# Attention strip of a two-layer graph network: f32 turns set singly among PV tiles, the 256-column product last in a tile, and the ELU's last two additions moved from GpSimd to VectorE

## The reference

```
q = h @ Wq.T + bq;  k = h @ Wk.T + bk;  v = h @ Wv.T + bv
scores = q @ k.T / sqrt(128);  scores = where(adj > 0, scores, -9e15)
att = softmax(scores) @ v
x = x + elu(att)
```

## Time and profile before

| | |
|---|---|
| time, median of 3 runs | 761.54 us (760.59 to 762.22) |
| the profiled execution's own time | 758.33 us |
| its span | 756.5 us |
| TensorE busy, matmuls | 724.9 us, 96% of the span |
| VectorE busy | 558.8 us, 74% |
| ScalarE busy | 549.0 us, 73% |
| GpSimd busy | 448.9 us, 59% |
| mean granted clock of TensorE | 0.975 |

### The profile page before, as it was taken

The page is one execution under the profiler, slowest core; times in us unless marked ns, Lnnn a source line. Parts: engine busy times, 40 slices in busy tenths (PEclk is TensorE's granted clock), DMA queues, the critical chain, the costliest instruction groups (busy, mean ns, idle before and its releaser), DMA issues. The chain is left out here.

```text
span 756.5 us, 18346 instructions
## 1 busy us (share of the span) xinstructions
PE 724.9 (96%) x6243; PEld 616.0 (81%) x6243; DVE 558.8 (74%) x1190; ACT 549.0 (73%) x1090; POOL 448.9 (59%) x388
## 2 busy tenths in 40 slices
PE   7989999999999999999999998989799999999996
PEld 5567878888888888888888887887688888888885
DVE  6979787887878778787787877578387477577572
ACT  4745868778786877878777787676986887887810
POOL 6688699999999999999999989470000000000000
PEclk9999999999999999999999999758999999999999
DMA  6299899998989889898898943783234542442100
GB/s 236 99 290 223 252 272 232 281 255 247 258 236 282 244 261 251 250 270 233 277 257 246 260 110 65 135 110 100 62 82 86 85 96 63 94 92 65 38 10 12
DMA packets 193307, 132.71 MB, mean 175 GB/s; under 512 B 174064, under 2 KB 180720, under 8 KB 184944
## 3 DMA queue, kind: packets, MB, share of 16 engines
q1 hardware_dynamic: 192528, 131.90, 65.6%
q10 hardware_dynamic: 576, 0.26, 0.1%
q0 software_dynamic: 160, 0.00, 0.0%
HBM read 71.31 MB, written 18.89 MB: 119 GB/s over the span
## 5 line engine op out<-in xcount | busy, mean ns | idle before, releaser
L898 DVE CUSTOM_DVE_ANT_0 scores<-ps_s,mask_both 128x1024 f32<-128x1024 f32 x128 | 155.8, 1217 | 17.4 <-POOL mask_both L350 17.4
L770 ACT ACTIVATE scores<-scores,neg_max 128x1024 f32<-128x1024 f32 x128 | 146.0, 1142 | 25.9 <-DVE neg_max L904 25.9
L917 DVE TENSOR_TENSOR low<-scores 128x1024 bf16<-128x1024 f32 x96 | 140.1, 1459 | 30.4 <-ACT scores L770 30.4
L350 POOL TENSOR_SCALAR mask_both<-mask_bytes 128x2048 bf16<-128x2048 uint8 x64 | 153.3, 2396 | 5.4 <-POOL mask_bytes L345 0.4
L345 POOL TENSOR_SCALAR mask_bytes<-adj_both 128x2048 uint8<-128x2048 int32 x64 | 148.3, 2336 | 2.9 <-DMA adj_both<-in_adj 2.0
L1152 PE MATMUL spare<-v_parts,hiT 128*128 128x256 bf16 x768 | 140.3, 273 | 1.6 <-DMA lowT<-low 1.6
L784 ACT ACTIVATE hiT<-spare 128x512 bf16<-128x512 bf16 (+1 forms) x128 | 103.0, 805 | 50.9 <-PE spare L1133 48.3
L1153 PE MATMUL spare<-v_parts,lowT 128*128 128x128 bf16 x768 | 133.5, 219 | 0.0
L1584 PE MATMUL ps_x<-q_parts,over_k 128*128 128x258 bf16 x1024 | 117.4, 276 | 3.6 <-issue 3.6
L1584 PEld LDWEIGHTS ps_x<-q_parts,over_k 128*128 128x128 fp8e4 x1024 | 99.8, 98 | 19.2 <-issue 3.7
L1106 PE MATMUL ps_s<-k_hi,q_strip 128*128 128x512 f32 x256 | 112.4, 439 | 2.1 <-PEq L81 1.9
(11 more groups left out here) (174 smaller groups left out, 1280.2 us busy)
## 6 DMA issues: line engine op xcount, KB each, us to landing
adj_both<-in_adj SPq DMA_DIRECT2D x64, 1024.0 KB, 5.3
mask_bytes_dram<-mask_bytes SPq DMA_DIRECT2D x32, 512.0 KB, 2.9
x_sb<-in_x SPq DMA_DIRECT2D x8, 256.0 KB, 6.8
out<-res SPq DMA_DIRECT2D x32, 64.0 KB, 1.6
lowT<-low SPq DMA_TRANSPOSE x96, 4.8
mask_both<-s_row_dram SPq DMA_DIRECT2D x1, 1024.0 KB, 7.6
mask_both<-s_row_dram SPq DMA_DIRECT2D x1, 768.0 KB, 11.4
over_k<-mask_bytes_dram SPq DMA_TRANSPOSE x16, 4.6
```

The costliest lines, as they stand in the source:

```text
L350: return nc.gpsimd.tensor_scalar(out, src, -NEG, NEG, ALU.mult, ALU.add)
L770: nc.scalar.activation(sc, sc, ACT.Exp, bias=neg_max[:, bn:bn + 1], accum_out=row_sum[:, bn, k:k + 1]).then_inc(exp_done, 1)
L898: nc.vector.tensor_tensor_reduce(out=scores[bn % 2][:, part(k)], in0=ps_s[k % 2][:], in1=mask[bn % 2][:, part(k)], scale=1.0, scalar=LOWES ...
L917: nc.vector.tensor_tensor(low[k][:], p, high_half(p), ALU.subtract).then_inc(low_done, 1)
```

## The change

On TensorE, `turn` takes the products of the strip before into itself where there is one (`times_before`): each of the four f32 turns is followed by the two products of one tile. The waits of those products (`wait_for_part`, formerly in `times_v`) stand ahead of the first turn. `t_done` is still given by the fourth turn, behind which one tile's products follow. In every tile but the first of a strip the 128-column product now comes first and the 256-column one last. On GpSimd `add_elu` keeps one addition, exp + positive part, and gives a new semaphore `elu_ready`. VectorE gets `add_x`, (that sum - 1) + x in one instruction, between `moments_of(s-3)` and `low_part(s+1, 0)`; it gives `epi_done`.

```diff
--- before.py
+++ after.py
@@ -520,7 +520,7 @@
             halves_added, att_ready, att_cut = sem("acc_halves_added"), sem("att_ready"), sem("att_cut")
             att_exp_ready, epi_done = sem("att_exp_ready"), sem("epilogue_done")
             m_stored = [sem("even_masks_stored"), sem("odd_masks_stored")]
-            own, pool_own = sem("vector_steps"), sem("pool_steps")
+            own, elu_ready = sem("vector_steps"), sem("elu_ready")
             sp_gate, pool_gate = sem("sync_gate"), sem("pool_gate")
             bn_done, tail_own = sem("moments_taken"), sem("tail_vector_steps")
             h_ready, h_by_vector = sem("h_ready"), sem("h_by_vector_ready")
@@ -684,12 +684,8 @@
 
                     def add_elu(s):
 
-                        steps = Steps(pool, pool_own, 2 * s)
                         pool.wait_ge(att_exp_ready, s + 1)
-                        steps.do(nc.gpsimd.tensor_tensor(att_exp[:], att_exp[:], ones[:], ALU.subtract))
-                        steps.do(nc.gpsimd.tensor_tensor(att_exp[:], att_exp[:], att_pos[:], ALU.add))
-                        xs = x_sb[:, s, :] if isinstance(s, int) else x_sb[:, bass.ds(s, 1), :].rearrange("p o f -> p (o f)")
-                        nc.gpsimd.tensor_tensor(xs, xs, att_exp[:], ALU.add).then_inc(epi_done, 1)
+                        nc.gpsimd.tensor_tensor(att_exp[:], att_exp[:], att_pos[:], ALU.add).then_inc(elu_ready, 1)
 
                     make_bytes(0, 1)
                     make_mask(0, 1)
@@ -923,6 +919,13 @@
                         wait(dve, acc_out, s - 1)
                         nc.vector.reciprocal(inv_by_parity[:, b % 2:b % 2 + 1], inv_sum[:, b % 2:b % 2 + 1]).then_inc(inv_ready, 1)
 
+                    def add_x(s):
+
+                        dve.wait_ge(elu_ready, s + 1)
+                        xs = x_sb[:, s, :] if isinstance(s, int) else x_sb[:, bass.ds(s, 1), :].rearrange("p o f -> p (o f)")
+                        nc.vector.scalar_tensor_tensor(out=xs, in0=att_exp[:], scalar=-1.0, in1=xs,
+                                                       op0=ALU.add, op1=ALU.add).then_inc(epi_done, 1)
+
                     def moments_of(s):
 
 
@@ -1041,6 +1044,8 @@
                         if has(c, b, -3):
                             dve.wait_ge(epi_done, s - 2)
                             moments_of(s - 3)
+                        if has(c, b, -2):
+                            add_x(s - 2)
                         if isinstance(c, int) and s == T - 3:
                             dve.wait_ge(var_made, 1)
                             first_guess(FIRST)
@@ -1055,6 +1060,7 @@
                     inverse_sum(T - 1, 3)
                     dve.wait_ge(epi_done, T - 2)
                     moments_of(T - 3)
+                    add_x(T - 2)
                     dve.wait_ge(epi_done, T - 1)
                     moments_of(T - 2)
                     aggregate(slice(LAST.start, T - 1))
@@ -1108,14 +1114,22 @@
                             last = nc.tensor.matmul(o, rest, k_hi[:, col], start=False, stop=True)
                         last.then_inc(s_ready, 1)
 
-                    def turn(s, b, i):
+                    def turn(s, b, i, times_before):
+
 
                         pe.wait_ge(exp_done, 4 * s + 1)
-                        wait(pe, hiT_ready, 4 * (s - 1) + 2 + i)
+                        if times_before:
+
+                            wait_for_part(s - 1, 6 + i)
                         for t in range(4):
                             col = 512 * (6 + i) + D * t
-                            last = nc.tensor.transpose(ps_t[i % 3][:, D * t:D * t + D], scores[b % 2][:, col:col + D], ident[:])
-                        last.then_inc(t_done, 1)
+                            turned = nc.tensor.transpose(ps_t[i % 3][:, D * t:D * t + D], scores[b % 2][:, col:col + D], ident[:])
+                            if t == 3:
+                                turned.then_inc(t_done, 1)
+                            if times_before:
+                                last = tile_times_v(6 + i, t)
+                        if times_before:
+                            last.then_inc(pv_done, 1)
 
                     def turn_high(s, b, u):
 
@@ -1133,7 +1147,7 @@
                             last = nc.tensor.transpose(out[:, D * t:D * t + D], high[:, D * t:D * t + D], ident_half[:])
                         last.then_inc(t_done, 1)
 
-                    def times_v(s, i):
+                    def wait_for_part(s, i):
                         j = PV_ORDER[i]
                         if i < 2:
                             pe.wait_ge(pT_low_ready, 2 * s + i + 1)
@@ -1143,15 +1157,32 @@
                                 pe.wait_ge(lowT_in[j // 2], 16 * s + 16)
                         if i == 0:
                             wait(pe, acc_out, s)
+
+                    def tile_times_v(i, n):
+
+
+                        j = PV_ORDER[i]
+                        t = 4 * j + n
+                        first, final = i == 0 and n == 0, i == NC - 1 and n == 3
+                        if j >= 6:
+                            high, rest = (m[j - 6][:, D * n:D * n + D] for m in (pT_high, pT_low))
+                        else:
+                            high, rest = hiT[j // 2][:, D * (t % 8):D * (t % 8) + D], lowT[j // 2][:, t % 8, :]
+
+                        def times_low():
+                            return nc.tensor.matmul(ps_a[:, 0, :], rest, v_parts[:, t, 0, :], start=False, stop=False)
+
+                        if not first:
+                            times_low()
+                        last = nc.tensor.matmul(ps_a[:], high, v_parts[:, t, :, :], start=first, stop=final)
+                        if first:
+                            last = times_low()
+                        return last
+
+                    def times_v(s, i):
+                        wait_for_part(s, i)
                         for n in range(4):
-                            t = 4 * j + n
-                            if j >= 6:
-                                high, rest = (m[j - 6][:, D * n:D * n + D] for m in (pT_high, pT_low))
-                            else:
-                                high, rest = hiT[j // 2][:, D * (t % 8):D * (t % 8) + D], lowT[j // 2][:, t % 8, :]
-                            nc.tensor.matmul(ps_a[:], high, v_parts[:, t, :, :], start=(i == 0 and n == 0), stop=False)
-                            last = nc.tensor.matmul(ps_a[:, 0, :], rest, v_parts[:, t, 0, :], start=False,
-                                                    stop=(i == NC - 1 and n == 3))
+                            last = tile_times_v(i, n)
                         last.then_inc(pv_done, 1)
 
                     for k in range(NP):
@@ -1162,19 +1193,15 @@
                     def period(c, b):
                         s = 4 * c + b
                         before, ahead, ahead2 = has(c, b, -1), has(c, b, 1), has(c, b, 2)
-                        turn(s, b, 0)
+                        turn(s, b, 0, before)
                         if not ahead:
                             pe.wait_ge(masked, 4 * T)
                             turn_h(0)
-                        if before:
-                            times_v(s - 1, 6)
                         if ahead:
                             make_scores(s + 1, 1 - b % 2, 2)
-                        turn(s, b, 1)
+                        turn(s, b, 1, before)
                         if not ahead:
                             turn_h(1)
-                        if before:
-                            times_v(s - 1, 7)
                         if ahead:
                             make_scores(s + 1, 1 - b % 2, 3)
                         turn_high(s, b, 0)
```

## The result

The changed kernel takes **777.46 us** (median of 4 runs, 774.8 to 781.6), the kernel before beside it 761.88 (760.59 to 763.1): a ratio of **1.0209**, 95% interval 1.0171 to 1.0247. It is slower, clear of the noise, but the interval begins at 1.7%, so that it is not shown to be slower by as much as 2%. The prediction was 781.5 us with a range of 774 to 787, 88% on slower. The profiled execution took 781.6 us, with a span of 779.8 against 756.5 before.

A forecast was written before the change was run, and what follows sets the result against it. TensorE's gapless work and an equally long ScalarE-VectorE-ScalarE loop, 13.35 us a period, were taken as the bound; +21.6 - 0.8 - 0.8 = +20.0 on the median 761.54 gave 781.5 us, range 774 to 787.

The forecast's parts named there:

- Two loops of one length: Attention stage: the loop ScalarE to VectorE to ScalarE is as long as TensorE's period, 13.35 us.
- Who starts first holds the other: VectorE's subtraction against GpSimd's instruction: the first to start runs, the other stands; a held subtraction ends 1.07 us after.
- rival 1: VectorE keeps its turn: low_part(s,1) stays ahead of the mask half, TensorE sets 13.13 a period, 753.3 us; chance 8%.
- The loop, +0.77 a period: VectorE's loop: low_part(s,1) held, +1.25; low_part(s,2) freed, -0.48; over 28 periods +21.6 us.
- `add_x` worth 0 on the loop: VectorE's added instruction costs between 0.28 and 0.28 + 1.90 us, covered by 1.8 of idle time: 0.
- TensorE's waits: TensorE, with 0.99 us over a period, waits some 0.8 to 1 us for the second pT_low.
- The products' order, 0.22 a period but hidden: TensorE: the 256-column product last covers the scores' f32 load, 0.22 us a period, worth nothing under the longer loop.
- The single turns, worth 0: TensorE's f32 turns: each lasts 0.11 us itself, so spreading them saves 0; if load-bound, 0.44 a period.
- The end of the stage, -0.8 and -0.8: Last strips: ScalarE's wait for att goes, -0.8; shorter GpSimd additions before VectorE's moments, -0.8.
- Rival 2: VectorE keeps its turn and turns are load-bound: TensorE needs 12.69, the loop of 12.87 sets the pace, 746.5 us; chance 2%.
- Rival 3: add_x costs as well: 0.2 us a period, 787 us; worst, it and low_part(s+1,0) both held, +59; chance 8%.
- Rival 4: GpSimd's late work lengthens the loop only every other period: +9.2, 770.7 us; chance 4%.

The follow-up runs named there:

- Number 7: The changed kernel with TensorE's order as before the change and two GpSimd waits, behind turned_low(s,0) and behind low_part(s+1,0): 758.21 us, ratio 0.9948.
- Number 2: Only the TensorE part of the change (single turns, 256-column product last), add_elu as in the kernel before: 759.3 us, ratio 0.9966.
- number 4: The changed kernel with two unneeded 128x128 instructions on GpSimd around the remaining addition, so its mask half starts later: 784.64 us, ratio 1.0291.
- number 3: The changed kernel with one more GpSimd wait: the first mask half waits until VectorE has done turned_low(s,0): 767.24 us, ratio 1.0074.
- number 6: Number 5 with the four f32 turns issued together again, the 256-column product still last in a tile: 755.15 us, ratio 0.9898.
- number 1: Only the GpSimd and VectorE part of the change, TensorE's order as in the kernel before: 782.19 us, ratio 1.0241.
- number 5: Number 3 with a second GpSimd wait: the second bytes half waits until VectorE's low_part(s+1,0) is done: 753.39 us, ratio 0.9888.

## Why the prediction was right, point by point

**Two loops of one length.** Right. Number 7 leaves TensorE's work as it was and frees the loop: 13.34. Number 2 shortens TensorE's work and leaves the loop: 13.30. The period before was 13.34, so the loop lay 0.04 under TensorE's need. TensorE alone could give only 0.04 a period, and a longer loop had to show in full.

**Who starts first holds the other.** Right, and it carried the result. `low_part(s,1)` ends 1.07 after the mask half, the figure taken from the earlier trace rows, and the second mask half 1.76 after the subtraction (244.12 against 242.36). In the Trainium skill, SBUF — State Buffer, the section "SBUF: two separate sides" says the same as a rule: an exclusive lock between a GpSimd instruction that reads SBUF and a VectorE instruction with two SBUF inputs, which whoever starts first keeps for the whole instruction. The ten traces agree but for ties. A subtraction or `add_x` starts inside a mask half or bytes half, with 0.2 us or more of it left, 445 times in them. It is held 443 times, the closest with GpSimd 0.042 us ahead. The other two are the meetings of number 4 at 0.015 and 0.012 us, which VectorE won. So VectorE does win near ties, as rival 1 supposed, but nowhere from 0.042 us on; in the changed kernel GpSimd leads by 0.49.

**The loop, +0.77 a period.** Measured 0.734 (20.55 / 28). Of the two terms, the hold was worth +1.26 (2.48 against 1.22) for +1.25, and the freed `low_part(s,2)` -0.49 for -0.48. Walked through as the prediction walked it, the loop of period 13 is 0.61 + 0.61 + 4.15 + 2.56 + 0.03 + 6.11 = 14.07, so the other small difference is ScalarE's stretch, 6.11 where it was 6.16. Once in four periods (s = 12, 16 and so on, behind the loop's jump) the hold is 2.23 instead of 2.48, with a period of 13.84 behind one of 14.29; the two together are as long as any other two.

**`add_x` worth 0 on the loop.** Right in its effect. Its price within the bounds of 0.28 and 2.18 came out at 1.77, near the upper one. I had GpSimd's bytes halves at 194.9 and 196.8 and left open which one is met; it was the second. The cover held: `low_part(s+1,0)`, behind it, had stood 0.85 for ScalarE before and 0.2 in a hold, and now has neither. The exclusion of "both are held" was right for this kernel by a margin that the prediction did not state. Numbers 3 and 4 show how thin: the first bytes half starts 7.4 us behind the first copy in the changed kernel, 8.4 in a period of number 4 with the double hold and 9.0 in number 3.

**TensorE's waits.** Foreseen 0.8 to 1 us a period in front of the second `pT_low`; the table has 23.1 us in 28 waits, 0.83 each. GpSimd's wait for `att_exp` was to be 2 to 3 us and was 3.1.

**The products' order, 0.22 a period but hidden.** Right on both counts: 0.22 in number 6 against 7, and next to nothing (number 1 against after, 14.07 against 14.08) under the longer loop. The sign that the prediction gave for it was wrong: the second scores product was to start 0.28 to 0.30 behind the last product of a tile, and it is 0.34 (201.24 to 201.58 in number 5, 244.73 to 245.07 in the changed kernel). The prediction's own durations, 0.11 for a 256-column product and 0.23 for the first scores product, give 0.34.

**The single turns, worth 0.** Right, 0.016 a period in number 6. The rule of the Trainium skill that the prediction weighed against the row, TensorE: Matmul & The Clock Gate, section LDWEIGHTS, would have made it 0.44. Four turns in a row can't tell a turn's own time from that of its load. Set singly, each turn's load has a 256-column product to stand behind, and the pace is still 0.11 us: it is the turn's own.

**The end of the stage, -0.8 and -0.8.** Measured -0.96 from strip 30 to 31, where the row of ScalarE's wait for `att` is gone, and -1.14 from strip 31 to the last `att`. The terms were mis-sized by 0.2 and 0.3, both on the side that I took too small.

**The rest.** Two stretches that the prediction took as unchanged are not: +2.5 us in the first two periods and +1.9 in the second layer. The first holds one 4.3 us wait of TensorE for `lowT` (in the table of waits above). It is scatter of the opening. `add_elu` and `add_x` first come in period 2, so number 1 has the instructions of the kernel before in these two periods, and took 31.29 us for them against 28.45; number 4 has those of the changed kernel, and took 26.32 against 30.96. The second is in a stage where no instruction differs, and there too the ten executions scatter, from 274.4 us (number 1) to 276.8 (numbers 2 and 7), again not by kernel. Part of it is the clock. The same two stretches of 20 us, counted from the last `att`, before (from 60.2 us behind it) and after (columns as in the earlier trace rows):

```profile
542.00:562.00 20.00, 15.09 (x124) 12.46 (x123) 15.85 (x28) 17.69 (x33) 0.00 (x0) 0.91 0.26 58
```

```profile
563.35:583.35 20.00, 15.09 (x111) 11.92 (x110) 15.78 (x28) 16.18 (x30) 0.00 (x0) 0.83 0.26 57
```

TensorE gets through 124 matmuls before and 111 after, at a granted clock of 0.91 and 0.83: in both it idled for 4.9 us of the 20, and came back to full clock later in the second (in its four stretches of 5 us the clock is 1.00, 0.66, 1.00, 1.00 before and 1.00, 0.51, 0.81, 1.00 after). That is scatter that no term of a sum can hold; a profiled execution differs from another by 2 us for it.

**The size as a whole.** The forecast of +20.0 us is that of the profiles, less their scatter: loop and tail together are +18.45. The medians say +15.6, and the interval of the ratio reaches from 13.0 to 18.8, so +20.0 lies a little above it and the 20.55 of the loop less the tail's gains just inside. Of the 4.4 us by which the medians fall short of +20.0, the loop's term (21.6 against 20.55) and the tail's (1.6 against 2.1) make 1.5. The other 2.9, between 18.45 and 15.6, can't be placed, since the unprofiled runs have no trace; number 1, with the same loop to 0.01 us a period, had +20.3.

**The rivals.** None came in the changed kernel. Rival 1's time, 753.3, is what number 5 gives (753.39), but by two ordering waits and not by the 0.5 us of delay that the rival named as its point. Rival 2 falls with the single turns. Rival 3's worst order appears in number 3, but at 13.68 a period, 0.8 above the 12.87 of rival 1's loop, where the rival had 2.1. `add_x` and the hold of `low_part(s+1,0)` come to 1.89 + 1.68 = 3.6 there and not 4.1. And the prediction's 1.8 us of idle time leaves out a third piece, in front of the mask that follows the maximum. Before the change and in number 3 (where the `gate` is that mask's first step):

```profile
195.36 1.22 DVE L898 CUSTOM_DVE_ANT_0 scores<-ps_s,mask_both 128x1024 f32<-128x1024 f32 x1 [0.73 <-POOL mask_both L350]
```

```profile
200.02 0.06 DVE L894 MEMSET gate<- 128x1 f32 x1 [0.20 <-PE spare L1148]
```


VectorE stood 0.73 us there for GpSimd's mask and now stands 0.20. That leaves some 0.3 of the difference unplaced. Rival 4's alternation appears in number 4, which is worse than the rival had it: not one free period and one lengthened by 1.5, but one near 13.0 and one of 15.3 to 16.4.

## What to carry to other kernels

Work taken from an engine that shares something with the one on the critical path is a change of phase before it is a saving: list where the two meet, who starts first at each meeting and by how much, and redo that list with the new times. Where a meeting matters, order it by a wait on the engine that has time to spare; two such waits turned this change from +2.1% into -1.1%. When one meeting is moved, look at the next: number 3 repaired the first and lost at the second.

## What the runs showed of the hardware that was not expected

- A 128x128 `SCALAR_TENSOR_TENSOR` with both inputs in SBUF is held as fully as the large subtraction: 0.28 us free, 1.77 in the changed kernel, 1.89 in number 3. Here a small instruction put between large ones of the other engine cost 1.6 of the 1.9 us that one of theirs takes.
- Starting first by the trace's stamps does not decide at the very closest: at leads of 0.015 and 0.012 us GpSimd's mask half was held by the subtraction behind it (number 4), at 0.042 and more it never was. No meeting lies between.
- Holding feeds back. In number 4 short and long periods follow each other (12.98 and 15.28, 13.03 and 16.35) though every period issues the same instructions: an early subtraction makes GpSimd late, which makes the next subtraction late.
- Two executions can differ by 4.6 us in the opening (26.3 and 31.0 us for the first two periods) and by 2.4 in the second layer (274.4 to 276.8 us) with the same instructions there. The medians of kernels whose loops agree to 0.34 us in all (the change and number 1) lie 4.7 us apart.
